# Deformable convolution: samples from image rows and row steps as stationary operands

## What is computed

```
off = conv2d(x, ow, ob).reshape(Bn, K, 2, Hh, Ww)          # K = 9 taps
cy = iy + dy + off[:, :, 0];  cx = ix + dx + off[:, :, 1]
y0, x0 = floor(cy), floor(cx);  wy, wx = cy - y0, cx - x0
samp = (gather(y0, x0, (1-wy)*(1-wx)) + gather(y0, x0+1, (1-wy)*wx)
        + gather(y0+1, x0, wy*(1-wx)) + gather(y0+1, x0+1, wy*wx))
out = einsum('bckhw,ock->bohw', samp, w) + b
h = relu(group_norm1(out)) + x
```

## Time and profile before

| | before |
|---|---|
| median of 3 runs | 748.67 us (747.22 to 749.94) |
| the profiled execution | 753.67 us |
| its span | 751.7 us |
| instructions on TensorE | 13,258 matmuls, 13,258 weight loads |
| busy share of the span: PE, PEld, DVE, ACT, POOL | 79%, 56%, 81%, 65%, 20% |
| DMA moved | 111.16 MB |

### The profile page before, as it was taken

The page is one execution under the profiler, slowest core; times in us unless marked ns, Lnnn a source line. Parts: engine busy times, 40 slices in busy tenths (PEclk is TensorE's granted clock), DMA queues, the critical chain, the costliest instruction groups (busy, mean ns, idle before and its releaser), DMA issues.

```text
span 751.7 us, 29125 instructions
## 1 busy us (share of the span) xinstructions
PE 593.7 (79%) x13258; PEld 417.2 (56%) x13258; DVE 608.8 (81%) x791; ACT 489.6 (65%) x736; POOL 150.6 (20%) x258
## 2 busy tenths in 40 slices
PE   2629999999886988888894977588888899386681
PEld 1216887766444766556672743467666666255350
DVE  6998999924279999999997425999999999785446
ACT  2876674233139899999974215879999998422514
POOL 1014000010452323444100143222344410000000
PEclk9959999999997899999997989889999999778696
DMA  5003000000798888888600269688888860000002
GB/s 208 0 23 93 3 4 19 4 3 23 202 324 293 265 311 277 263 262 257 256 4 2 54 173 370 235 288 279 268 263 252 265 241 2 3 3 3 2 3 113
DMA packets 30198, 111.16 MB, mean 148 GB/s; under 512 B 11140, under 2 KB 15940, under 8 KB 25976
## 3 DMA queue, kind: packets, MB, share of 16 engines
q0 software_dynamic: 14912, 87.85, 35.0%
q1 hardware_dynamic: 15160, 21.42, 9.5%
HBM read 92.25 MB, written 19.65 MB: 149 GB/s over the span
## 4 chain that ended last, share of the span: by engine, by line
PE 36%; DVE 30%; ACT 13%; DMA 9%; issue 7%; SPq 4%; POOL 0%; DVEq 0%; ACTq 0%; POOLq 0%
PE psum L1382 11%; PE psum L1436 6%; PE psum L1470 5%; DVE arena L809 5%; DVE arena L810 5%; PE psum L1585 4%; DVE arena L811 4%; DMA offsets<-arena 4%; DMA arena<-offsets_by_batch 3%; SPq L511 3%; ACT arena L1188 2%; ACT arena L1187 2%; ACT arena L1198 2%; ACT arena L1178 2%; PE psum L1592 2%
## 5 line engine op out<-in xcount | busy, mean ns | idle before, releaser
L1470 PE MATMUL psum<-arena 64*64 64x297 f32 (+4 forms) x4512 | 236.3, 357 | 44.8 <-DVE arena L811 29.2
L1470 PEld LDWEIGHTS psum<-arena 64*64 64x64 f32 x4512 | 176.5, 143 | 111.7 <-DVE arena L811 54.2
L1671 POOL DMA_DIRECT2D arena<-offsets_by_batch x128 | 82.5, 658 | 208.5 <-DVE arena L811 137.8
L1436 PE MATMUL psum<-arena 32*32 32x512 f32 x2304 | 90.9, 665 | 23.4 <-issue 17.5
L809 DVE SCALAR_TENSOR_TENSOR arena<-arena 128x792 f32<-128x792 f32 (+3 forms) x96 | 92.4, 962 | 5.7 <-ACT arena L1188 4.7
L1198 ACT ACTIVATE arena<-psum 128x792 f32<-128x792 f32 (+1 forms) x96 | 83.0, 865 | 20.3 <-PE psum L1470 11.4
L1382 PE MATMUL psum<-arena 32*32 32x512 f32 x2592 | 93.6, 597 | 0.0
L810 DVE SCALAR_TENSOR_TENSOR arena<-arena 128x792 f32<-128x792 f32 (+3 forms) x96 | 92.1, 959 | 0.0
L811 DVE SCALAR_TENSOR_TENSOR arena<-arena 128x792 f32<-128x792 f32 (+3 forms) x96 | 92.1, 959 | 0.0
L1188 ACT ACTIVATE arena<-arena 128x792 f32<-128x792 f32 (+3 forms) x96 | 84.7, 883 | 0.0
L1187 ACT ACTIVATE arena<-arena 128x792 f32<-128x792 f32 (+3 forms) x96 | 84.6, 881 | 0.0
(11 more groups left out here) (162 smaller groups left out, 691.6 us busy)
## 6 DMA issues: line engine op xcount, KB each, us to landing
arena<-offsets_by_batch POOLq DMA_DIRECT2D x112, 576.0 KB, 8.0
arena<-offsets_by_batch POOLq DMA_DIRECT2D x16, 624.0 KB, 7.7
offsets<-arena SPq DMA_DIRECT2D x32, 256.0 KB, 10.5
offsets_by_batch<-offsets SPq DMA_DIRECT2D x184, 24.0 KB
arena<-columns POOLq DMA_DIRECT2D x24, 160.0 KB, 9.6
columns<-arena POOLq DMA_DIRECT2D x8, 320.0 KB, 6.8
arena<-in_x SPq DMA_DIRECT2D x4, 512.0 KB, 5.4
out<-arena SPq DMA_DIRECT2D x8, 256.0 KB, 2.2
```

The source lines that it names most:

```text
L1436: ins = t_.matmul(ps_q(2 * axis + h, conv_bank(m) + i), cols(W_CONV[L] + (axis * K + t) * Q, Q, Q * i, Q), ap(XA + (BLK * m + 8 * h + t // ...
L1470: ins = t_.matmul(ps_t(s, bank + r, first * K * w, many * K * w), window, ap(g_at(unit, d0) + first * TW + s * w, [[GS + TW, many], [SLOTS ...
L1671: g.dma_start(cols(in_at(n, 0), 2 * in_rows(n) * W, 64 * r + 32 * half, 32), bass.AP(batch_d.tensor, 2 * (4 * r * NB + n) * INS, [[0, QW / ...
```

## The change

The weight of the own row is written as one minus the two others, so a sample is: (tent) x (own row) plus (positive part of y) x (tent) x (step to the row below) plus (negative part) x (tent) x (step from the row above).

- The y-terms are gone, and the third product. VectorE makes two products per unit, max(y,0) and min(y,0) times the tent, directly from the loaded offsets; it waits itself for a free ring slot (`s_un`).
- The tent, in the batch's buffer, becomes a moving operand as it is. So the buffer is free when the samples are done: `load_batch` (and SP's loads of the reach at the end) wait on `s_un` where they waited on `s_g`.
- There are two sets of stationary operands: image rows (`v_at`, a ring of 8, spread by ScalarE alone in four instructions) and steps between rows (`d_at`, a ring of 9). VectorE subtracts neighbouring rows into a small tile DC, waits for it (`s_dc`), and spreads two image groups; ScalarE spreads the other two. Where the ring of nine turns over inside a batch, each spread is split in two. At the image's edges the step is the row itself.
- `sample` has five steps p (20 products of one or two rows) and between them four image rows (16 products of one row): 36 products.
- `copy_samples` changes the sign. A chunk of windows is nine rows, not eight.

```diff
 sp.wait_ge(s_fd, 16 * (L + 1))
-sp.wait_ge(s_g, UNITS * L + NU * (NB - 2))
+sp.wait_ge(s_un, UNITS * L + NU * (NB - 2))
 ...
 # vector: batch
-dve.wait_ge(s_nd, UNITS * L + unit + 1)
-v.scalar_tensor_tensor(term(0), term(0), 0.0, part(tx), ALU.min, ALU.mult)
-v.scalar_tensor_tensor(term(1), term(1), 1.0, part(tx), ALU.subtract, ALU.mult)
-v.scalar_tensor_tensor(term(2), part(ty), 0.0, part(tx), ALU.min, ALU.mult).then_inc(s_g, 1)
-if u == 1 and 1 <= n < NB - 1:
-    spread_windows(L, n + 1)
+if unit >= RING:
+    dve.wait_ge(s_un, UNITS * L + unit - RING + 1)
+v.scalar_tensor_tensor(term(0), part(ty), 0.0, part(tx), ALU.max, ALU.mult)
+v.scalar_tensor_tensor(term(1), part(ty), 0.0, part(tx), ALU.min, ALU.mult).then_inc(s_g, 1)
+if u == 1 and n + 1 < NB:
+    spread_steps(L, n + 1)
+
+def spread_steps(L, n):
+    c = n // 2
+    dve.wait_ge(s_zc[c % 2], 64 * (NCHUNK // 2 * L + c // 2 + 1))
+    dve.wait_ge(s_zd, NB * L + n)
+    dve.wait_ge(s_un, UNITS * L + NU * max(n - 1, 0))
+    rows = SLOTS if n < NB - 1 else SLOTS - 1
+    row = lambda k: ap(chunk_at(n, SLOTS * n) + k * C, [[ZCB, NBK], [C, rows], [1, C]])
+    ins = v.tensor_tensor(ap(DC, [[DCB, NBK], [C, rows], [1, C]]), row(1), row(0), ALU.subtract)
 ...
+    ins.then_inc(s_dc, 1)
+    dve.wait_ge(s_dc, NB * L + n + 1)
+    for i in range(2):
+        for window, row_ in step_views(n, i):
+            ins = v.tensor_scalar(window, row_, con("image4", i, 1), None, ALU.mult)
+    ins.then_inc(s_zv, 1)
 ...
 # scalar
+def spread_rows(L, n):
 ...
+    for i in range(4):
+        ins = a.activation(*row_views(n, i), ACT.Copy, scale=con("image4", i, 1))
     ins.then_inc(s_za, 1)
+def spread_steps(L, n):
+    act.wait_ge(s_dc, NB * L + n + 1)
+    for i in (2, 3):
+        for window, row in step_views(n, i):
+            ins = a.activation(window, row, ACT.Copy, scale=con("image4", i, 1))
+    ins.then_inc(s_zd, 1)
 ...
 copy_samples(L, unit)
 n, u = divmod(unit, NU)
-if unit + RING < UNITS:
-    y_terms(L, unit + RING)
+if u == 0 and n + 1 < NB:
+    spread_steps(L, n + 1)
 if u == NU - 1 and n + 2 < NB:
+    spread_rows(L, n + 2)
     distances(L, n + 2)
-    spread_windows(L, n + 2)
 ...
 # tensor: sample
-for p in rows_:
-    first = max(p - 1 - SLOTS * n, 0)
-    d0 = first - (p - 1 - SLOTS * n)
-    many = min(p + 1 - SLOTS * n, SLOTS - 1) - first + 1
+for p in range(-1, SLOTS):
+    first, many = max(p, 0), 1 if p in (-1, SLOTS - 1) else 2
     for s in range(2):
         for r in range(2):
-            window = cols(z_at(p, 2 * u + s), 64, 64 * r, 64)
+            window = cols(d_at(SLOTS * n + p, 2 * u + s), 64, 64 * r, 64)
 ...
+    if p < SLOTS - 1:
+        for s in range(2):
+            for r in range(2):
+                ins = t_.matmul(ps_t(s, bank + r, (p + 1) * K * w, K * w),
+                                cols(v_at(SLOTS * n + p + 1, 2 * u + s), 64, 64 * r, 64),
+                                ap(in_at(n, 0) + (p + 1) * W + u * TW + s * w,
+                                   [[SLOTS * W, K], [1, w]], 64 * r, 64),
+                                start=False, stop=False, skip_group_check=True)
 ...
 # gpsimd: load_batch
 if n >= 3:
-    pool.wait_ge(s_g, UNITS * L + NU * (n - 2))
+    pool.wait_ge(s_un, UNITS * L + NU * (n - 2))
```

More of the change, by code:

```diff
@@ L51 @@
 KP = 16
-ZROWS = 12
+VROWS = 2 * SLOTS
+DROWS = 2 * SLOTS + 1
 NCHUNK = NB // 2
-CHUNKS = [(8 * c + 1 if c else 0, min(8 * c + 9, H)) for c in range(NCHUNK)]
+CHUNKS = [(8 * c, min(8 * c + 9, H)) for c in range(NCHUNK)]
 CHUNK_ROWS = 9
@@ L203, in build @@
         G = IN_AT[2] + INK
-        YA = G + RING * 3 * GS
+        DB = G + RING * 2 * GS
+        ZROW = NBK * 64
+        YA = DB + DROWS * ZROW
         XA = YA + N
@@ L211, in build @@
         ZB = SE + 2 * 3 * SX
[L212 to L213 removed]
+        DC = ZB + VROWS * ZROW
+        DCB = SLOTS * C
+        ZC = DC + NBK * DCB
         ZCB = CHUNK_ROWS * C
@@ L427, in g_at, with v_at, d_at, chunk_at @@
         def g_at(unit, d):
[L429 to L456, removed]
+            return G + (unit % RING * 2 + d) * GS
+        def v_at(row, blk):
+            return ZB + row % VROWS * ZROW + blk * 64
+        def d_at(row, blk):
+            return DB + (row + 1) % DROWS * ZROW + blk * 64
+        def chunk_at(n, row):
+            return ZC + n // 2 % 2 * ZCS + (row - CHUNKS[n // 2][0]) * C
+        def row_views(n, i):
+            return (ap(v_at(SLOTS * n, 0) + i * C, [[64, NBK], [ZROW, SLOTS], [1, C]]),
+                    ap(chunk_at(n, SLOTS * n), [[ZCB, NBK], [C, SLOTS], [1, C]]))
+        def step_views(n, i):
+            first = SLOTS * n
+            turn = min(SLOTS, DROWS - (first + 1) % DROWS)
+            views = [(ap(d_at(first + a, 0) + i * C, [[64, NBK], [ZROW, b - a], [1, C]]),
+                      ap(DC + a * C, [[DCB, NBK], [C, b - a], [1, C]])) for a, b in ((0, turn), (turn, SLOTS)) if a < b]
+            if n == 0:
+                views.append((ap(d_at(-1, 0) + i * C, [[64, NBK], [1, C]]), ap(chunk_at(0, 0), [[ZCB, NBK], [1, C]])))
+            return views
         def row_parts(bank, s, rho, y, rows):
@@ L1178, in distances @@
                 a.activation(tx, tx, ACT.Abs, bias=con("minus_q")).then_inc(s_u, 1)
-            def y_terms(L, unit):
-                n, u = divmod(unit, NU)
-                if unit >= RING:
-                    act.wait_ge(s_un, UNITS * L + unit - RING + 1)
-                part = ap(in_at(n, 1) + u * TW, [[W, in_rows(n)], [1, 2 * WB[u]]])
-                term = lambda d: ap(g_at(unit, d), [[TW, in_rows(n)], [1, 2 * WB[u]]])
-                a.activation(term(0), part, ACT.Copy, scale=-1.0)
-                a.activation(term(1), part, ACT.Abs).then_inc(s_nd, 1)
             def copy_samples(L, unit):
@@ L1224, in _ @@
                 distances(L, 0)
-                for unit in range(RING):
-                    y_terms(L, unit)
-                spread_windows(L, 0)
+                spread_rows(L, 0)
+                spread_steps(L, 0)
                 copy_offsets(L, 3)
+                spread_rows(L, 1)
                 distances(L, 1)
-                spread_windows(L, 1)
                 act.wait_ge(s_xs[0], 64 * (L + 1))
@@ L1467, in sample @@
                         for s in range(2):
                             for r in range(2):
-                                window = cols(z_at(p, 2 * u + s), 64, 64 * r, 64)
+                                window = cols(d_at(SLOTS * n + p, 2 * u + s), 64, 64 * r, 64)
                                 ins = t_.matmul(ps_t(s, bank + r, first * K * w, many * K * w), window,
-                                                ap(g_at(unit, d0) + first * TW + s * w,
+                                                ap(g_at(unit, first - p) + first * TW + s * w,
@@ L1472, in sample @@
                                                    [[GS + TW, many], [SLOTS * TW, K], [1, w]], 64 * r, 64),
-                                                start=(p == rows_[0]), stop=(p == rows_[-1]), skip_group_check=True)
-                                if (n, p) in ((0, 0), (NB - 1, H - 1)):
+                                                start=(p == -1), stop=(p == SLOTS - 1), skip_group_check=True)
+                                if edge:
                                     ins = t_.matmul(ps_t(s, bank + r, KR * w, 3 * w), window,
-                                                    ap(g_at(unit, 0 if n == 0 else 2) + KR * TW + s * w,
+                                                    ap(g_at(unit, 0 if n == 0 else 1) + KR * TW + s * w,
```

35 lines of the change are left out of this document (16 added, 19 removed).

## The result

| | before | after |
|---|---|---|
| median | 748.6 us (747.22 to 749.94) | 778.4 us (776.34 to 782.24) |
| the profiled execution, its span | 753.67, 751.7 us | 777.56, 775.5 us |
| matmuls on TensorE | 13,258 | 15,658 |

The change makes the kernel slower, by a factor of 1.040 (95% interval 1.036 to 1.045): 29.8 us between the medians, 23.8 us between the two profiled spans. The forecast was 785 us.

The account below looks back on a forecast made before the run. The prediction took VectorE as the bound before and TensorE's instruction stream beside the loads after. The two layers' +19.4 and +17.1 us, 36.5 us on a median of 748.67, gave 785 us (770 to 805, chance 0.48; wider range 728 to 828).

Parts of the forecast that it names:

- The beat: Time per batch of four image rows in both deformable layers, forecast at about 11.8 us, against about 10.1 before.
- The block's time of 6.65 us: Time TensorE takes per 256 instructions when the DMA engines are full, a mean of 7.3, 6.2 and 6.5 us.
- 4.24 plus 2.4 times the share: Forecast time in us of a 256-instruction block on TensorE while sampling, rising in proportion to the DMA share.
- The ends of the layers: Ends of the two deformable layers, forecast at 413.4 us (+19.4) and 657.0 us (+17.1).
- VectorE: VectorE's work per batch, forecast to fall from 9.86 to 7.85 us: 2.62 removed, 0.6 added.
- ScalarE: ScalarE's work per batch, forecast to fall from 9.9 to about 7.7 us: 4.4 removed, 2.2 added.
- TensorE's own pace: TensorE's array work per batch, forecast at 8.4 us, with splitting products costed at nothing in array time.
- The loads' ring: Cycle of offset loads, distances and sampling: two batches cannot take less than 19.4 us, so 9.7 us a batch.
- Waits in most batches: Sign that the forecast is wrong: ScalarE's distances wait for a DMA in most batches, pointing to rival two.
- rival two: Instruction stream hidden, offset loads limit the batch to 9.7 us: 729 us; with partial stops, 725 to 748, chance 0.17.
- The first: Rival: instruction stream stays hidden and TensorE's array sets the pace, 8.5 us a batch, 698 us; chance 0.10.
- The third: Rival: instruction stream starves TensorE and its clock falls too, 13.2 us a batch, 822 us; chance 0.18.

Follow-up runs that it names:

- e2: The kernel before with 12 extra products of four columns in each unit (48 more instructions, results unread): 789.6 us.
- e3: The kernel after with its offset loads cut to 256 of 4608 columns a partition from batch 3 on: 696.9 us.
- e6: The kernel before with only the later load release of the change (waiting for TensorE's samples, not VectorE's products): 758.0 us, ratio 1.011.
- e8: The kernel after with its offset loads cut to 2304 of 4608 columns a partition from batch 3 on: 719.3 us.
- e5: The kernel after with the same bytes loaded in transfers of 64 partitions and one axis, rows half as long: 864.3 us, 1.153 of before.
- e9: The kernel after with the same bytes loaded in two transfers of 64 partitions and both axes for a batch: 876.8 us.
- e12: The kernel of e5 with loads from batch 3 on taken from input x, each partition reading a row of its own: 847.4 us.
- e4: The kernel after with the third and fourth transfer of each load waiting for one more sampled unit: 797.2 us, 1.069 of before.

## Why the prediction came out right

**The sign and the cause** were right: the issue waits, at block ends inside units, are what the changed kernel waits for (28.4 of 28.4 us idle), and e2 and e3 show the two halves of the cause.

**The beat.** Forecast 11.8 us, measured 11.8 in the first layer and 12.0 in the second. The block's time of 6.65 us, from a stretch with share 1.0, and the model "4.24 plus 2.4 times the share" gave 6.0 at the share of 0.74 that came; measured 5.92. But the line between the two ends is wrong: at 0.49 it gives 5.4 (measured 4.66), at 0.89 it gives 6.4 (measured 7.30). The forecast hit since it was used in the middle, which was luck. The end at a share of 1.0 was not a packet's time alone either: of the three blocks behind the 6.65 us, the one of 7.3 held 6.05 us of busy TensorE where the others held 4.50, and the clock of that stretch was 0.85.

**The ends of the layers** were off, as these rows of TensorE's timeline show (first sample of the second batch, last of the last, in each layer):

```profile
240.00 0.40 PE L1481 MATMUL psum<-arena 64*64 64x99 f32 x8 [1.09 <-DVE arena L818]
...
405.02 0.32 PE L1486 MATMUL psum<-arena 64*64 64x30 f32 x5
...
494.77 0.61 PE L1481 MATMUL psum<-arena 64*64 64x99 f32 x8 [4.32 <-DVE arena L818]
...
663.99 0.32 PE L1486 MATMUL psum<-arena 64*64 64x30 f32 x5
```

| | forecast | measured |
|---|---|---|
| second batch starts, first layer | 243 | 240.0 |
| first layer ends | 413.4 (+19.4) | 405.3 (+11.3) |
| second layer, from the first one's end to its own | 263.0 (+17.1) | 259.0 (+13.1) |

The layers together are 24.4 us longer between the profiled executions, where I had 36.5. Three sizes were off. The second batch began 3 us earlier than forecast in both layers: TensorE was waiting for VectorE there (1.09 and 4.32 us in the rows above), not for its own blocks of batch 0. The thirteen batches from there took 145.6 us in the first layer (240.0 to 385.6) and 150.8 in the second, 11.2 and 11.6 each, not 11.8, because the early ones were faster: 9.2 us from clipping to clipping (three from 236.69 to 264.15 us; blocks of 5.4 us from 232 to 264). The last two took more than the 17 us forecast: 19.7 and 18.7. Batch 14 still has a load beside it, the DMA share from 380 us on being 0.33, and one more stop for issue, 2.64 us; it took 11.0 us, and batch 15 8.7, near the 8.5 forecast. Against the 12 us too much (36.5 less 24.4) stand 6 too little: the profiled execution of before lay 5.1 us above its median and that of after 0.8 us under its own, so that the medians are 29.8 us apart, not 23.9. That the two errors cancel in part is luck. So 785 was 6.6 us too long. The forecast range has a slip at its lower end: with the same sum a beat of 11 us gives 764 us, not 770.

**VectorE**: 7.85 us forecast; 90.43 busy us over 128 / 11.8 batches are 8.3. The subtraction took 0.55 where I had 0.45, and a split spread 1.14 where one in one piece takes 0.75; I had 0.15 more for it. **ScalarE**: 7.7 forecast, 7.9 by the same reckoning. Both cost nothing here, being off the path.

**TensorE's own pace**: 8.4 forecast, at most 8.6 measured (e3). That splitting products costs no array time held to within these 0.2 us.

**The loads' ring** was mis-sized. "At a beat of 11.8 us the later load is hidden" is right for TensorE, though the distances waited for their DMA 14 times of 32. Waits in most batches I had named as a sign of rival two; fewer than half is short of it, and the sign was badly chosen, since ScalarE had slack for these waits. A ring of 9.7 us would have cost the kernel before nothing, where e6 shows 8 us.

**The rivals.** The first (698 us) is what happens with small loads (696.9), the second (729) nearly what happens without the added instructions (735.6). The Trainium skill, page "Runtime: NRT & Kernel Launch", section "Instruction fetch mechanics", says that a boundary between blocks is mostly hidden; here that holds at a DMA share of 0.18 (4.39 us a block) and fails from 0.71 on (5.9 us and more). The third came in small: the granted clock of the steady stretch was 0.95, a mean between the two levels of 1.2 and 2.4 GHz. Four times it fell to the lower one, at the end of a stop of 2.25 to 4.34 us or just after it, for 13.6 us in all; after the stop that ended at 367.15 us, the windows line of 368 to 370 us has:

```profile
368.00:370.00 2.00, 2.00 (x39) 2.00 (x35) 1.27 (x2) 0.30 (x1) 0.00 (x0) 0.50 1.03 433
```

That is a part of the beat that my sum did not have. Against e3 a batch is 3.2 us longer, of which 2.3 are idle time and 0.9 are more busy time of TensorE (99.57 us over 128 / 11.8 batches are 9.2, in e3 106.44 over 110 / 8.6 are 8.3). How much of the 0.9 the clock costs was not told apart; an estimate from the 13.6 us at half clock is 0.6 us a batch at most. With longer stops the clock was lower (1.00 in e3 and e8, 0.87 in e5); how much of e5's time is the clock's wasn't told apart either.

## What to carry to other kernels

Before splitting products, count TensorE's instructions per unit of time and not only its columns: 256 instructions came in one packet, and beside heavy loads a block of 256 took 6 to 7 us here, in e2 as in the kernel after, though e2's added products were of four columns. A kernel close to that has a bound that no engine's busy share shows; the stops for "issue" after 128 matmuls, in a stretch of the trace with full DMA engines, are the sign to look for. The gain of the change is there (697 us with small loads), but only beside fewer loaded bytes; none of the kernels here with the 36 products and the full loads was faster than the one before.

## What the runs showed of the hardware that I had not expected

- Transfers of 64 partitions kept the DMA engines busy 0.87 to 0.89 of the time at 193 to 206 GB/s (e5, e9, e12); those of 32 and 16 partitions 0.71 to 0.76 at 219 to 247 GB/s, with the same bytes. Length of rows and reading one row 16 times were excluded as the cause; a single row took about twice as long (1.41 us against 0.69).
- Spacing the transfers (e4) did not shorten a block: 5.92 us both ways in the first layer, 6.37 against 6.02 in the second.
- A stop for issue ended 1.2 to 1.9 us after a packet of instructions had come in (39 of 39 in the kernel after), and the packet itself took 0.9 to 1.8 us, hardly more than in e3 (0.9 to 1.5).
- Up to a DMA share of 0.49 the loads cost TensorE 0.3 us a block (4.66 against 4.39), though at 0.74 they cost 1.5 us.
